# Making the last layer's keys and values for all batches in the head and ramp, and keeping them in the MLP's buffer

## The reference

```python
x = x + (attention(ada_ln(x) @ Wq, ada_ln(ctx) @ Wkv) @ Wp + bp)            # CROSS0
x = x + gate_a * (attention(modulate(ln(x)) @ W_qkv) @ W_proj + b_proj)      # SELF1
x = x + (attention(ln(x) @ W_qc, ln(ctx) @ W_kvc) @ W_cproj + b_cproj)       # CROSS1
x = x + gate_m * (gelu(modulate(ln(x)) @ W_mlp1 + b_mlp1) @ W_mlp2 + b_mlp2)
```

## Time and profile before

| what | us |
|---|---|
| median of 3 runs | 305.57 (304.89 to 306.3) |
| the profiled execution's own time | 304.43 |
| its span | 302.6 |
| TensorE busy | 262.3 |
| VectorE busy | 220.9 |
| ScalarE busy | 215.6 |
| GpSimd busy | 142.5 |

### The profile page before, as it was taken

How to read it: one execution, slowest core, us unless ns; L and a number is a source line. 1 busy time by engine, 2 the same in 40 slices (tenths; PEclk the granted TensorE clock), 3 DMA queues, 4 the chain that set the end, 5 groups by cost and what they waited for, 6 DMA issues and landing times.

```text
span 302.6 us, 10070 instructions
## 1 busy us (share of the span) xinstructions
PE 262.3 (87%) x3781; PEld 171.4 (57%) x3781; DVE 220.9 (73%) x448; ACT 215.6 (71%) x396; POOL 142.5 (47%) x296
## 2 busy tenths in 40 slices
PE   2636659999999999999999999999999999889895
PEld 2313335666666666565666666666666565555764
DVE  6972896997779787797887988879978886311622
ACT  2126248697977969779687786877869788899640
POOL 7590846626336173263754837547263545420500
PEclk9985758999999999999999999999999999999999
DMA  6993332344343454443423234233332200000111
GB/s 199 266 247 73 104 79 75 87 124 110 107 120 101 130 129 96 125 112 90 108 63 102 75 89 107 62 87 83 100 103 61 57 5 5 3 0 2 52 54 35
DMA packets 34223, 27.44 MB, mean 91 GB/s; under 512 B 4904, under 2 KB 33920, under 8 KB 34176
## 3 DMA queue, kind: packets, MB, share of 16 engines
q1 hardware_dynamic: 31776, 24.81, 31.1%
q10 hardware_dynamic: 2400, 1.99, 2.7%
HBM read 6.46 MB, written 1.06 MB: 25 GB/s over the span
## 4 chain that ended last, share of the span: by engine, by line
PE 56%; DVE 15%; ACT 14%; issue 7%; POOL 2%; DMA 2%; SPq 1%; ACTq 1%; POOLq 0%; DVEq 0%
PE all_ps L500 10%; PE all_ps L438 9%; PE score_ps L463 8%; DVE neg_max L881 7%; ACT normed L657 6%; PE keyed_ps L486 6%; PE all_ps L511 5%; PE all_ps L531 4%; PE all_ps L446 3%; PE all_ps L523 3%; PE all_ps L428 3%; PE all_ps L542 3%; DVE rest L873 3%; ACT parts L671 2%; ACT attn_t L708 2%
## 5 line engine op out<-in xcount | busy, mean ns | idle before, releaser
L881 DVE TENSOR_REDUCE neg_max<-score_ps 128x8 f32<-128x1024 f32 x96 | 116.9, 1218 | 12.7 <-PE score_ps L463 11.9
L691 ACT ACTIVATE probs<-keyed_ps 128x1024 f32<-128x1024 f32 x96 | 98.3, 1024 | 18.9 <-PE keyed_ps L486 18.9
L500 PE MATMUL all_ps<-probs,values 128*32 128x128 f32 x1536 | 61.2, 278 | 0.5 <-ACT probs L691 0.5
L463 PE MATMUL score_ps<-stack_k,stack_q 62*128 62x128 bf16 x768 | 39.4, 224 | 11.1 <-DVE neg_max L881 10.7
L500 PEld LDWEIGHTS all_ps<-probs,values 128*32 128x32 f32 x1536 | 36.3, 109 | 18.7 <-issue 8.9
L1056 POOL CAST max_parts<-neg_max 128x16 bf16<-128x16 f32 x48 | 9.7, 203 | 69.3 <-DVE neg_max L881 69.3
L463 PEld LDWEIGHTS score_ps<-stack_k,stack_q 62*128 62x128 bf16 x768 | 22.4, 96 | 33.4 <-DVE neg_max L881 21.7
L486 PE MATMUL keyed_ps<-stack_q,stack_k 64*128 64x128 bf16 x768 | 38.4, 220 | 0.7 <-ACT probs L691 0.7
L1041 POOL TENSOR_TENSOR rstd<-var_eps,minus_half 128x4 f32<-128x4 f32 x24 | 24.5, 1020 | 25.3 <-DVE var_eps L846 24.9
L873 DVE SCALAR_TENSOR_TENSOR rest<-all_ps,bcol_p,parts 128x512 f32<-128x512 f32 x24 | 18.0, 750 | 21.8 <-ACT parts L671 21.8
L438 PE MATMUL all_ps<-normed_t,w_qk 128*128 128x512 f32 x48 | 30.3, 721 | 1.9 <-ACT normed_t L643 1.9
(11 more groups left out here) (101 smaller groups left out, 393.5 us busy)
## 6 DMA issues: line engine op xcount, KB each, us to landing
stack_q<-parts SPq DMA_DIRECT2D x72, 128.0 KB, 2.5
stack_k<-parts SPq DMA_DIRECT2D x66, 128.0 KB, 2.4
gate<-gate_d SPq DMA_DIRECT2D x16, 128.0 KB, 3.4
stack_q<-max_rows SPq DMA_DIRECT2D x96, 4.0 KB
xs<-in_x_dram SPq DMA_DIRECT2D x4, 256.0 KB, 7.2
cs<-in_ctx_dram SPq DMA_DIRECT2D x4, 256.0 KB, 6.6
out_dram<-xs SPq DMA_DIRECT2D x8, 128.0 KB, 1.8
stack_k<-parts ACTq DMA_DIRECT2D x6, 128.0 KB, 4.5
```

Source lines behind the costliest of these rows:

```text
L463: mm = pe.matmul(score_ps[:, e, a * T:(a + 1) * T], stack_q[rows, g % STACKS, CP * c + a, cols], stack_k[rows, g % STACKS, CP * c + a, col ...
L500: mm = pe.matmul(ps[QUAD * a:QUAD * (a + 1), c * T:(c + 1) * T], values[:, u // PER % STACKS, u % PER * PAIRS + CP * c + a, 2 * e:2 * e + ...
L691: act.activation(probs[:, n % 3, :], keyed_ps[:, :, :].rearrange("t e n -> t (e n)"), ACT.Exp, scale=float(D) ** -0.5).then_inc(probs_read ...
L881: dve.tensor_reduce(neg_max[:, u % 2, :, CP * c:CP * (c + 1)], score_ps[:, :, :].rearrange("t e (a k) -> t e a k", k=T), AX.X, ALU.max, ne ...
```

## The change

1. For each of the context's four groups i, keys and values of CROSS1 are made early. At tick `PRE_AT[i]` (-6, -5, -1, 3) GpSimd makes the root (`context_root`) and ScalarE normalises the context into `hidden` (`normalise_context`); three ticks later TensorE transposes it and ScalarE copies it back (`turn_context`, `keep_turned`); four ticks later TensorE projects keys and values and ScalarE copies both out (`project_context`, `keep_context`). They stay in `hidden` until their group is due.
2. In CROSS1 the context's normalisation, its transposes, `modulate` and both projections are gone. `first_part` and `copy_values` read `hidden`, and `leave_rest` subtracts two tensors of SBUF.
3. The head: SyncE loads tokens 0 and 1 and the bias rows, stacks group 0, and only then loads the rest. ScalarE issues its eight later loads (`load_rest`) after the first `modulate`, clears the value buffers and permutes the bias rows, both of which GpSimd did. VectorE normalises both inputs of group 1, fills both key stacks and takes unit 0's maxima ahead of tick -6.
4. The order inside a tick is another on all engines, and the MLP's tables are.

```diff
-        UP_AT = (41, 43, 44, 45, 46, 46, 46, 48, 48, 48, 49, 49, 52, 53, 53, 53)
-        DOWN_AT = (49, 49, 50, 50, 51, 51, 53, 56)
-        GELU_AT = (48, 50, 51)
-        ADD_AT = (49, 50, 50, 51, 51, 51, 52, 53)
+        UP_AT = (41, 43, 44, 45, 46, 46, 47, 47, 47, 48, 48, 48, 52, 52, 52, 52)
+        DOWN_AT = (48, 49, 49, 50, 51, 52, 52, 56)
+        GELU_AT = (48, 49, 50)
+        ADD_AT = (49, 49, 50, 50, 50, 50, 51, 53)
+        PRE_AT = (-6, -5, -1, 3)
...
+        def own_keys(g):
+            return g if g is not None and layer(g) < CROSS1 else None
...
+            load_tokens(0, c_too=False)
+            for r, b in ((R_SSQ, L0_xcond_bss_q), (R_SSKV, L0_xcond_bss_kv), (R_Q[0], L0_xcond_bq),
+                         (R_K[0], L0_xcond_bkv), (R_Q[1], L1_xcond_b_qkv), (R_Q[2], L1_xcond_b_qc)):
+                sp.dma_start(brow[r:r + b.shape[0] // H, :], row(b)).then_inc(loaded["brow"], 16)
+            load_tokens(0, x_too=False)
+            load_tokens(1)
...
+            sp.dma_start(wqc[:, :], L1_xcond_W_qc).then_inc(loaded["wqc"], 16)
+            sp.dma_start(wkvc[:, :], L1_xcond_W_kvc).then_inc(loaded["wkvc"], 16)
+            load_tokens(2)
+            load_tokens(3)
...
+            def turn_context(i):
+                pe.wait_ge(pre_normed, i + 1)
+                ps = take("pnorm", i)
+                for j in range(PER):
+                    mm = pe.transpose(ps[:, j * T:(j + 1) * T], hidden[:, 0, i, j * T:(j + 1) * T], ident[:, :])
+                mm.then_inc(pre_turned_ps, 1)
+
+            def project_context(i):
+                pe.wait_ge(pre_turned, i + 1)
+                if i == 0:
+                    pe.wait_ge(w_permuted, 2 * 2)
+                    pe.wait_ge(loaded["wkvc"], 16)
+                pe.matmul(take("pk", i), w_qk[:, CROSS1, 1, :], hidden[:, 1, i, :], start=True, stop=True).then_inc(pre_ps, 1)
+                ps = take("pv", i)
+                for j in range(PER):
+                    mm = pe.matmul(ps[:, j * H:(j + 1) * H], hidden[:, 1, i, j * T:(j + 1) * T], wkvc[:, H:2 * H],
+                                   start=True, stop=True)
+                mm.then_inc(pre_ps, 1)
...
+            transpose_normed(1, 0)
+            transpose_normed(1, 1)
+            scores(0, 0)
+            scores(0, 1)
...
+            def clear_values(i):
+                v = values[:, i, :, :, :]
+                act.activation(v.rearrange("t u e d -> t (u e d)").rearrange("t (a n) -> t a n", n=128),
+                               ident[:, :].unsqueeze(1).broadcast_to([T, 16, 128]), ACT.Copy, scale=0.0).then_inc(values_ones, 1)
+                act.wait_ge(values_ones, 2 * i + 1)
+                act.activation(v[:, :, 0:4:3, D], ident[:, 0:64].rearrange("t (u e) -> t u e", e=2), ACT.Copy,
+                               scale=0.0, bias=1.0).then_inc(values_ones, 1)
+
+            act.wait_ge(consts_ready, 2)
+            clear_values(0)
+            act.wait_ge(loaded["brow"], 16 * 10)
+            act.activation(brow_p[:, :].rearrange("r (e d p) -> r e d p", e=2, d=D),
+                           brow[:, :].rearrange("r (p e d) -> r e d p", e=2, d=D), ACT.Copy).then_inc(rows_permuted, 1)
+
+            def load_rest():
+                act.dma_start(wp0[:, :], L0_xcond_Wp).then_inc(loaded["wp"], 16)
+                act.dma_start(wmod[:, :], L1_xcond_W_mod).then_inc(loaded["wmod"], 16)
+                for i, b in enumerate((L0_xcond_bp, L1_xcond_b_proj, L1_xcond_b_cproj)):
+                    act.dma_start(b_out[:, i, :], row(b).broadcast_to([128, H])).then_inc(loaded["bout"], 16)
...
+                if (s, n) == (CROSS1, 1):
+                    i = g - CROSS1 * (B // PER)
+                    act.wait_ge(pre_done, 2 * i + 2)
+                    act.activation(parts[:, g % 2, n, 0, :], hidden[:, 0, i, :], ACT.Copy).then_inc(hi_ready, 1)
+                    return
...
+            def normalise_context(i):
+                act.wait_ge(pre_root_ready, 3 * (i + 1))
+                b0 = PER * i
+                for j in range(PER):
+                    ins = act.activation(hidden[:, 0, i, j * T:(j + 1) * T], cs[:, b0 + j, :], ACT.Identity,
+                                         bias=pre_off[:, i, j:j + 1], scale=pre_rstd[:, i, j:j + 1])
+                ins.then_inc(pre_normed, 1)
+
+            def keep_turned(i):
+                act.wait_ge(pre_turned_ps, i + 1)
+                act.activation(hidden[:, 1, i, :], bank("pnorm", i), ACT.Copy).then_inc(pre_turned, 1)
+
+            def keep_context(i):
+                act.wait_ge(pre_ps, 2 * i + 1)
+                act.activation(hidden[:, 0, i, :], bank("pk", i), ACT.Identity,
+                               bias=bcol_p[:, R_K[2]:R_K[2] + 1]).then_inc(pre_done, 1)
+                act.wait_ge(pre_ps, 2 * i + 2)
+                act.activation(hidden[:, 1, i, :], bank("pv", i), ACT.Copy).then_inc(pre_done, 1)
+
             def copy_values(g):
+                i = g - CROSS1 * (B // PER)
+                if i >= 0:
+                    act.wait_ge(pre_done, 2 * i + 2)
+                    act.wait_ge(attn_done, 2 * PER * (g - STACKS + 1))
+                    act.activation(values[:, g % STACKS, :, 0:4:3, 0:D],
+                                   hidden[:, 1, i, :].rearrange("t (p e d) -> t p e d", e=2, d=D),
+                                   ACT.Copy).then_inc(v_ready, 1)
+                    return
...
+            clear_values(1)
...
+                if tick == -1:
+                    clear_values(2)
+                if tick in GELU_AT:
+                    activate_hidden(GELU_AT.index(tick))
+                g = front(tick, -10)
+                if g is not None and g > 1:
+                    normalise_act(g, 0)
+                g = attention(front(tick, -8))
+                if g is not None:
+                    first_part(g, 0)
                 if unit(tick - 1):
                     attn_with_bias(tick - 1)
...
+                if tick - 3 in PRE_AT:
+                    keep_turned(PRE_AT.index(tick - 3))
+                if tick - 4 in PRE_AT:
+                    keep_context(PRE_AT.index(tick - 4))
+                if tick - 0 in PRE_AT:
+                    normalise_context(PRE_AT.index(tick - 0))
...
+                if n == 1:
+                    dve.tensor_scalar(pre_var[:, g, :].rearrange("t (i j) -> t i j", j=2), st[:, :, 2:6:3],
+                                      1.0 / H, EPS[CROSS1], ALU.mult, ALU.add).then_inc(pre_var_ready, 1)
...
+                if (layer(g), n) == (CROSS1, 1):
+                    dve.wait_ge(split_ready, 2 * (2 * (g - 1) + n - 1))
+                    dve.tensor_tensor(rest[:, n, :], hidden[:, 0, g - CROSS1 * (B // PER), :], parts[:, g % 2, n, 0, :],
+                                      ALU.subtract).then_inc(rest_ready, 1)
+                    return
...
+            normalise(1, 0)
+            normalise(1, 1)
+            fill_stack(1)
+            fill_stack(2)
+            row_max(0, 0)
+            row_max(0, 1)
...
-            clear_values(0)
             inverse_root(1, 0)
             inverse_root(1, 1)
             split_rest(0, 0)
+            clear_stack(1)
```

More of the change, by code:

```diff
@@ L753, in _ @@
                     modulate(g, 0, True)
-                g = front(tick, -8, 1)
-                if g is not None:
-                    modulate(g, 1, True)
                 g = attention(front(tick, -7))
@@ L761, in _ @@
                 if g is not None:
+                    modulate(g, 1, True)
+                g = front(tick, -8, 1)
+                if g is not None:
                     modulate(g, 1, False)
@@ L778, in _ @@
                     copy_values(g)
-                g = attention(front(tick, -8))
-                if g is not None:
-                    first_part(g, 0)
         @block.vector
@@ L969, in _ @@
                     add_branch(tick - 2)
+                if unit(tick - 1):
+                    divide(tick - 1)
+                g = front(tick, -10, 1)
+                if g is not None and g > 1:
+                    norm_stats(g, 1)
                 g = attention(front(tick, -7))
@@ L995, in _ @@
                     leave_rest(g, 0)
-                for n in range(B // 2):
-                    if ADD_AT[n] == tick:
-                        add_mlp(n)
+                g = front(tick, -9, 1)
+                if g is not None and g > 1:
+                    normalise(g, 1)
         @block.gpsimd
@@ L1118, in _ @@
             split_rest(0, 0)
+            clear_stack(1)
             for tick in range(FIRST, LAST):
+                g = front(tick, -7)
+                if g is not None and g >= GROUPS:
+                    add_mlp_bias(g - GROUPS)
                 g = front(tick, -10)
```

241 lines of the change are left out of this document (120 added, 121 removed).

## The result

| | before | changed |
|---|---|---|
| median, us | 305.32 (304.89 to 306.3, 4 runs) | 315.34 (314.55 to 316.44, 4 runs) |
| profiled execution, us | 304.43 | 314.55 |
| its span | 302.6 | 312.7 |

The ratio is 1.0313, 95% interval 1.0279 to 1.0347. The change costs 10 us; the forecast was 311.3.

A forecast was written before the change was run, and what follows sets the result against it. TensorE, busy 87% of the span, was taken as the steady part's main bound, idling in the head and ramp. CROSS1 -2.6, order +1.0, ramp +3.5, ticks 0 to 7 +3.9: +5.8 on 304.43, 310.2; median 311.3, range 301 to 317.5.

The forecast's parts named there:

- CROSS1: Ticks 24 to 39: less TensorE work, limited by VectorE in tick 25; -0.65 us a group, -2.6 for four.
- ticks 0 to 7: Context groups 2 and 3 add TensorE and ScalarE work: +3.9 us, near the lower bound +3.5, upper +6.
- the tail: End of the kernel, up and down projections around the last group's statistics: 0, between -1.5 and +1.5 us.
- The ramp: Group 0's key stack to first exponential: ScalarE's new work and waits cost +3.5 us, bounds -1.1 and +7.7.
- I add up ScalarE, since everything new is on it: Ramp: ScalarE's pieces sum to 21.0 us, first exponential 1.1 earlier without waits; waits of 4.6 make it +3.5.
- The part ahead of 22.51 I set at 0: Head, before the last issue of group 0's key stack: no change, bounds -2 and +2 us.
- The order: Inside ticks: `attn_t` behind four normalisations every fourth tick costs 0.25 us; ticks 8 to 23 +1.0, bounds -1.6 and +2.4.
- Most swaps are between neighbours that are both ready; they get 0: New order inside ticks: most swaps cost nothing, between -0.4 and +0.6 us a cycle of four ticks.
- (A): Rival, faster: TensorE bounds CROSS1 and its 9.8 us return whole; sum -7.4, 298.2 us; chance 0.18.
- (B): Rival, dear ramp: half clock there (+7.7), full lump in ticks 0 to 7 (+6); 317.7 us; chance 0.15.
- (D): Rival, a wash: CROSS1 gives 6 us, the ramp costs 1.5; sum +0.4, 306.0 us; chance 0.12.
- (C): Rival: in CROSS1 `leave_rest` with two SBUF inputs stalls against GpSimd, four times 1.16 us; 315.9 us; chance 0.08.

The follow-up runs named there:

- experiment 8: Changed kernel without the early context, in the new order with the new head, gates two per tick: 308.1 us, ratio 1.0069 to the kernel before.
- experiment 2: Changed kernel with context groups 2 and 3 made at ticks 21 and 25 instead of -1 and 3: 312.96 us, ratio 1.0239.
- experiment 7: Changed kernel with the whole old order inside a tick, early context kept, gates two per tick: 316.61 us, ratio 1.032.
- experiment 12: As experiment 1, but value buffers 1 and 2 cleared on GpSimd again, not on ScalarE: 312.77 us, ratio 1.0247.
- experiment 9: New head and MLP tables only: no early context, old order inside a tick, gates two per tick: 304.11 us, ratio 0.9931 to the kernel before.
- experiment 10: As experiment 9, but gates one per tick as in the kernel before: 302.66 us, ratio 0.9902.
- experiment 1: Changed kernel with SyncE issuing the gates' spreads two per tick in ticks 3 to 10, not one in ticks 3 to 18: 312.98 us, ratio 1.0222.
- experiment 3: Changed kernel with ScalarE's `attn_t` back directly behind the second exponential: 314.74 us, ratio 1.032.
- experiment 4: Changed kernel with TensorE turning the maxima ahead of the sums again, ring of banks likewise: 315.22 us, ratio 1.0284.
- experiment 5: Changed kernel with the edits of experiment 3 and experiment 4 together, gates two per tick: 314.54 us, ratio 1.027.
- experiment 11: As experiment 10, but the second half of unit 0's row scores taken behind group 1's query projection on TensorE: 302.77 us, ratio 0.9884.

## Why the prediction was right and wrong

The sign and the range held: slower, 315.34 in 301 to 317.5, with 311.3 forecast. That the sum came within 4 us is in part luck. In the profiled execution CROSS1 is 1.0 us worse than forecast, ticks 8 to 23 4.4 worse (+5.4, beyond the upper bound of +2.4) and ticks 0 to 7 2.9 worse, while everything ahead of the first exponential is 2.4 better and the tail 1.7 better. By the medians, which come from several sets of runs and so hold to about 1 us, the 10 us are made up so: head and tables alone (gates two per tick) -1.4, the new order on top +4.0 (304.11 to 308.10), the early context on top +4.9 (to 312.98), the gates one per tick in that order +2.4 (to 315.34).

**CROSS1: the mechanism held, the size nearly.** Forecast -0.65 a group, measured -0.72 (18.41 for 19.13); tick 25 takes 5.09 where I had set 5.2, with VectorE as the releaser. Tick 26 got nothing of its +0.25, tick 27 got 0.31 that I had set at 0. TensorE's own loss is 2.2 us in ticks 24 and 25 (4.49 and 3.67 busy for 4.91 and 5.44), not 2.5. Within the new order the early context is worth more: experiment 8, without it, has a cycle of 19.49 us, so it saves 1.08 a group and the order takes 0.36 back. Over sixteen ticks it is -1.6, not -2.9, as ticks 33 and 34 were 1.2 longer than their likes; their mean granted clock is 0.83 and 0.86. Experiment 2 has them at 5.08 and 4.49, at full clock, so this is the clock's part (last section), not the change's. Experiment 7 adds what I had not seen: even this gain hangs on the new order.

**The ramp: the sum came close, in part by luck.** Forecast +3.5, measured +2.1 for the stretch (24.25 for 22.18), and ScalarE's busy time in it is 19.81 us where the sum had 21.0. (By its own terms the sum was 1.2 us under 22.18 before the waits, not 1.1.) The step "I add up ScalarE, since everything new is on it" holds for the last 6 us only. Up to 39.75 the chain of the changed kernel runs through TensorE and VectorE; from there on it is ScalarE's list, the second clearing in it. But a second chain, VectorE's maxima and GpSimd's offset for context group 2, is 0.26 us behind, so taking the clearings off ScalarE (experiment 12, 3.7 us) moved the first exponential by 0.15. The sum had no term for that chain. "The part ahead of 22.51 I set at 0" was the other miss: it got 0.9 us shorter. The two last issues of `load_rest` that I feared took 0.9 us, not 2.2. Without any early context the first exponential is at 44.48 in the new order (experiment 8) against 45.93; in the old order it is at 44.19 and 42.70 (experiments 9 and 10) against 47.50. Experiments 9 and 10 have the same head, so a difference of 1.5 us here is no more than executions differ by (last section).

**Ticks 0 to 7: right place, undersized.** The step "near the lower bound since neighbouring ticks take part of that lump" failed: +3.9 forecast, +6.8 measured. That this is beyond the upper bound of +6 hangs on the clock in tick 0: experiment 1, with a full clock there, has 44.75 us, +5.3. Ticks 1 to 7, which the clock left alone, take 6.1 more, ticks 3 and 7 alone 4.7. In tick 3 ScalarE goes straight from TensorE's two projections through three context pieces to the copy the next tick waits for:

```profile
67.48 0.72 ACT L761 ACTIVATE hidden<-all_ps,bcol_p 128x512 f32<-128x512 f32 x1
68.05 0.63 ACT L764 ACTIVATE hidden<-all_ps 128x512 f32<-128x512 f32 x1
68.64 1.65 ACT L751 ACTIVATE hidden<-cs,pre_off,pre_rstd 128x128 f32<-128x128 f32 x4
70.19 0.36 ACT L799 ACTIVATE summed<-all_ps 128x256 f32<-128x256 f32 x1
```

ScalarE takes its list in order, so the neighbouring ticks could have taken a part only if the code had put it there. Experiment 8 shows the cause: without the early context ticks 1 to 7 take 34.82 us, with it 40.32, where the kernel before takes 34.21. So 5.5 of 6.1 are the context's.

**The order: half the size, and half the mechanism.** Forecast +0.25 a cycle, measured about +0.5. I charged `attn_t` behind the normalisations; experiments 3 to 5 show that it and the sums' turning ahead of the maxima's each hold the ticks 4g+3 at 4.34. The other half, ticks 4g+1 at 5.91, goes away with the old order; TensorE's attention waits there 0.43 us for the bank that VectorE's rest frees (L541 behind L997), where the value projection filled the gap before. That this is the cause was read, not tested.

**Tick 19: the step that was missing.** "Most swaps are between neighbours that are both ready; they get 0" is the sentence that failed. One of them was not ready: GpSimd's key split went behind an addition that waits for a DMA. The wait (1.72 us) stood in the trace of before. Experiment 1 shows its price: 2.4 us of the median, and in single executions anything from 0.7 to 3.6 us.

**The rivals.** (A) fell: TensorE's wait in tick 25 is the 1.42 us shown. (B) fell by half: the mean clock in the ramp rose to 0.76, so that was not dear, but its full lump in ticks 0 to 7 came. (D) fell: CROSS1 gave 1.6, not 6. (C) named 315.9, next to the measured time, for a wrong reason. `leave_rest` with two SBUF inputs takes 0.79 to 0.855 us, where the form with PSUM takes 0.75, and no 1.16 us wait stands before it:

```profile
178.61 0.85 DVE L987 TENSOR_TENSOR rest<-hidden,parts 128x512 f32<-128x512 f32 x1 [0.20 <-ACT parts L742]
```

```profile
179.00 0.78 POOL L1238 TENSOR_TENSOR xs<-xs,branch 128x128 f32<-128x128 f32 x1
```

The Trainium skill, page "SBUF — State Buffer", section "Who interferes with whom", lets the two engines contend when such a pair overlaps. The trace agrees that they do: GpSimd's addition beside it takes 0.78 us, three times, instead of 0.454. The cost is 0.3 us on GpSimd and 0.1 on VectorE in each of these ticks, and tick 25 still ends as forecast.

**The tail** was set at 0, within 1.5: it gave 1.7. Experiment 10 has the new tables with the old order and already gives 1.0 of it (65.95 for 66.95), so 1.0 are the tables' and 0.7 the order's.

## What to carry to other kernels

Moving work off the busiest engine pays only up to the next engine in the same stretch: here 7.7 us of TensorE's work bought 1.6 to 2.9, because VectorE's maxima bounded that tick, and cost 5.5 in ticks 1 to 7, where half of it was put. When an instruction is moved on an in-order engine, look at what waits ahead of its new place, not only at whether its own inputs are ready; a wait that was free stops being free once something useful stands behind it. And when undoing a suspect changes nothing, undo it together with the next: two causes may each be enough.

## What was not expected of the hardware

TensorE's clock after a short wait is not the same from execution to execution. In the changed kernel and in experiment 1 TensorE waits the same 2.21 us ahead of unit 0's second scores. In the first, tick 0 then has a mean granted clock of 0.71, and the query projection takes 2.07 us; in the second, the clock stays at 1.00 and it takes 1.12. Tick 0, changed kernel and experiment 1:

```profile
45.84:51.73 5.89, 4.83 (x59) 2.31 (x60) 1.68 (x3) 4.30 (x10) 1.08 (x4) 0.71 0.05 11
```

```profile
45.93:50.32 4.39, 3.33 (x59) 1.84 (x60) 0.59 (x2) 4.20 (x10) 0.41 (x2) 1.00 0.01 2
```

That is 1.5 us without any difference in the code near it. It may be part of why this execution of experiment 1 took 309.49 us and the others 312.7 to 313.3, of which there is no profile. What decides it was not tried. The kernel before has 0.77 in its tick 0, so a part of this cost is in it as well. In experiment 2 TensorE waits 2.58 us at the end of tick 25, and all of tick 26 is at half clock (0.50): there the wait is paid twice. In the changed kernel ticks 25 and 33 have nearly the same waits for VectorE's maxima, and only in the second the clock fell (1.00 and 0.83).

VectorE's cast of group 0's keys, in the head, takes 0.56 to 0.67 us in four profiled executions (experiments 4, 10, 11 and 12) and 3.08 or 3.09 in the nine others with the new head. Experiments 9 and 10 have the same head, and differ here first by when VectorE gets to it:

```profile
16.65 3.08 DVE L1070 CAST parts<-rest 128x512 bf16<-128x512 f32 x1
```

```profile
16.14 0.56 DVE L1069 CAST parts<-rest 128x512 bf16<-128x512 f32 x1
```

In the first GpSimd's subtraction had begun at 16.56, just ahead of the cast, and its clearing of a stack ran on to 19.45; the cast ended at 19.73. In the second the cast was over before that subtraction, which began at 16.50. From there on TensorE's work of the head comes 1.4 to 1.8 us earlier in experiment 10, and the first exponential at 42.70, not 44.19. With the early context the short cast gains nothing: experiment 4 has it, and its first exponential is at 46.13.
